# Routing the first half of the tokens first, and splitting the attention's weights inside the tile loop

## The reference

```python
x = x + 0.5 * ffn(layernorm(x), gate_w, expert_bias, w_up, w_down)
x = x + attention(layernorm(x), Wq, bq, Wk, bk, Wv, bv, Wo, bo)
x = x + 0.5 * ffn(layernorm(x), gate_w, expert_bias, w_up, w_down)
```

## Time and profile before

| what | value |
|---|---|
| three timed runs | 1325.23, 1333.52, 1334.07 us; median 1333.52 us |
| the profiled execution | 1327.57 us, its span 1325.8 us, granted clock 0.921 |
| TensorE busy | 926.0 us (70%) |
| VectorE busy | 1061.2 us (80%) |
| ScalarE busy | 677.8 us (51%) |
| GpSimd busy | 765.7 us (58%) |
| chain that ended last | VectorE 38%, TensorE 22%, GpSimd 15%, issue 15%, ScalarE 8% |

### The profile page before, as it was taken

One profiled execution on the slowest core, in us unless ns is written; L12 is line 12 of the kernel. 1 busy time (PEld: TensorE's weight loads), 2 busy tenths in 40 slices (PEclk: granted clock), 3 DMA queues, 4 the chain that ended last, 5 costly groups with the idle time before them and its releaser, 6 DMA issues.

```text
span 1325.8 us, 32789 instructions
## 1 busy us (share of the span) xinstructions
PE 926.0 (70%) x12808; PEld 753.3 (57%) x12808; DVE 1061.2 (80%) x2172; ACT 677.8 (51%) x950; POOL 765.7 (58%) x635
## 2 busy tenths in 40 slices
PE   4204978778876877877877887877978777767800
PEld 3203967666665655655655665655756567666700
DVE  7886766888899999899999998999998666447734
ACT  2113746556655655655655665645756464545500
POOL 2277627517767557557556564557978612766154
PEclk9999998999989999999999998988989888979865
DMA  9322424310000000000000000000000012233131
GB/s 331 128 92 88 126 68 106 84 45 6 10 6 7 8 6 8 7 6 7 8 6 2 2 2 2 2 2 17 14 13 14 29 53 69 85 113 100 54 87 52
DMA packets 69508, 61.77 MB, mean 47 GB/s; under 512 B 8304, under 2 KB 60016, under 8 KB 69104
## 3 DMA queue, kind: packets, MB, share of 16 engines
q1 hardware_dynamic: 60448, 42.64, 10.3%
q0 software_dynamic: 8192, 16.79, 4.1%
q10 hardware_dynamic: 720, 0.23, 0.1%
HBM read 30.80 MB, written 28.84 MB: 45 GB/s over the span
## 4 chain that ended last, share of the span: by engine, by line
DVE 38%; PE 22%; POOL 15%; issue 15%; ACT 8%; DMA 1%; DVEq 0%; POOLq 0%; ACTq 0%; SPq 0%
POOL xs L634 7%; DVE arena_a L1209 5%; DVE arena_c L1214 4%; PE bank L963 3%; DVE arena_b L1257 3%; ACT arena_b L1131 3%; DVE xn_new L424 2%; DVE arena_c L1273 2%; POOL arena_b L663 2%; PE bank L965 2%; PE bank L964 2%; PE bank L740 2%; DVE arena_c L1218 2%; PE bank L742 2%; PE bank L741 2%
## 5 line engine op out<-in xcount | busy, mean ns | idle before, releaser
L634 POOL DMA_INDIRECT xs<-xhl,slot_idx x128 | 154.5, 1207 | 102.7 <-issue 56.5
L800 ACT ACTIVATE arena_c<-bank,s_pre 128x1024 f32<-128x1024 f32 x92 | 102.6, 1115 | 204.0 <-PE bank L742 203.9
L1361 POOL TENSOR_TENSOR arena_a<-arena_a 128x1024 f16<-128x1024 f32 x64 | 139.0, 2171 | 55.5 <-ACT arena_a L1137 54.9
L1343 POOL TENSOR_TENSOR arena_a<-arena_b,trig_rows 128x512 f32<-128x512 f32 x128 | 160.1, 1271 | 6.8 <-issue 6.8
L825 DVE SCALAR_TENSOR_TENSOR arena_c<-arena_c,s_h 128x1024 f16<-128x1024 f32 x92 | 128.8, 1400 | 30.3 <-ACT arena_c L805 30.3
L1137 ACT ACTIVATE arena_c<-arena_a 128x1024 f16<-128x1024 f32 x64 | 67.6, 1057 | 164.3 <-DVE arena_a L1209 164.3
L663 POOL DMA_INDIRECT arena_b<-ys,slot_idx x96 | 106.9, 1113 | 75.5 <-DMA ys<-arena_b 47.9
L755 PE MATMUL bank<-wdn_hi,arena_c 128*128 x736 | 135.3, 226 | 20.1 <-DVE arena_c L825 20.1
L740 PE MATMUL bank<-arena_b,wup_hi 128*128 128x256 f16 x368 | 107.4, 292 | 59.2 <-DVE arena_b L821 59.2
L756 PE MATMUL bank<-wdn_hi,arena_c 128*128 x736 | 135.1, 226 | 0.0
L757 PE MATMUL bank<-wdn_lo,arena_c 128*128 x736 | 134.9, 225 | 0.0
(11 more groups left out here) (224 smaller groups left out, 3755.9 us busy)
## 6 DMA issues: line engine op xcount, KB each, us to landing
arena_b<-xs SPq DMA_DIRECT2D x92, 128.0 KB
ys<-arena_b SPq DMA_DIRECT2D x92, 128.0 KB
xs<-arena_c SPq DMA_DIRECT2D x2, 3072.0 KB, 18.4
arena_a<-in_w_up SPq DMA_DIRECT2D x1, 2048.0 KB, 13.0
arena_b<-in_w_down SPq DMA_DIRECT2D x1, 2048.0 KB, 13.5
xs<-xhl,slot_idx POOLq DMA_INDIRECT x128, 2.3
out_x<-x_tok SPq DMA_DIRECT2D x8, 256.0 KB, 2.6
arena_b<-ys,slot_idx POOLq DMA_INDIRECT x96
```

Source lines behind the costliest of these rows:

```text
L634: nc.gpsimd.indirect_dma_start(d["xs"][half], bass.IndirectOffsetOnAxis(slot_idx[:, half, choice, t:t + 1], axis=0), xhl[:, half, t, :], N ...
L1343: i = nc.gpsimd.tensor_tensor(q_trig[h], q_relu[h], trig_rows[:, bass.ds(u * BLK, BLK)], ALU.mult)
L1361: nc.gpsimd.tensor_tensor(q_lo, arena_a[:, 0:2 * BLK], q_hi, ALU.subtract).then_inc(a["q_lo_done"], 1)
```

## The change

1. In the prologue TensorE, ScalarE and VectorE take the first half's four blocks through transposes, gate products, split, gating and `route`, and then the second half's. `route_product(0)` writes to another PSUM bank, since the second half's logits lie in the old one.
2. The weights' largest values are taken on VectorE behind each half's route, no longer ahead of the gate; both low splits of the experts' weights follow the second half's route.
3. GpSimd reduces the up weights' largest values over the partitions behind 4 tiles of half 0's scatters (8 DMAs), those of the down weights behind 13 (26 DMAs), those of the attention behind all scatters of both halves.
4. The scale `s_y` is applied to the copied result of the down product, no longer to the gate's weights.
5. The attention's twelve pieces go into the tile loop of half 0, behind the low part of tiles 2, 4, 6, 8, 14, 15, 16, 17, 18, 19, 20 and 21. The rows of two biases are loaded into `arena_b` after the down weights are split, and TensorE waits for all logits ahead of `route_product(1)` only.

```diff
@@ buffers
-        bk_row, bv_row = take(HD), take(HD)
...
+        bk_row, bv_row = arena_b[:, 2 * HD:3 * HD], arena_b[:, 3 * HD:4 * HD]
@@ first_transpose
-            for n in range(NBLK):
-                pe.wait_ge(first_norm, n + 1)
...
-            for n in range(NBLK):
-                pe.wait_ge(first_hi, n + 1)
...
+            for half in range(2):
+                blocks = range(half * NBLK // 2, (half + 1) * NBLK // 2)
+                for n in blocks:
+                    pe.wait_ge(first_norm, n + 1)
...
+                for n in blocks:
+                    pe.wait_ge(first_hi, n + 1)
...
@@ first_copy, first_logits
-            for n in range(NBLK):
+            for n in range(half * NBLK // 2, (half + 1) * NBLK // 2):
@@ gating
-                then(nc.vector.scalar_tensor_tensor(w12[:, 0, tiles], col(2), s_y[:, 0:1], col(5), ALU.mult, ALU.mult))
-                then(nc.vector.scalar_tensor_tensor(w12[:, 1, tiles], col(4), s_y[:, 0:1], col(5), ALU.mult, ALU.mult))
+                then(nc.vector.tensor_tensor(w12[:, 0, tiles], col(2), col(5), ALU.mult))
+                then(nc.vector.tensor_tensor(w12[:, 1, tiles], col(4), col(5), ALU.mult))
@@ route_product, route
+        def ps_route(i):
+            return ps_tr if i else bank[0][:, 0, :]
@@ ffn_pe
                 route_product(pe, 0)
+                pe.wait_ge(gate_read, NBLK)
                 route_product(pe, 1)
@@ ffn_dve
-                nc.vector.tensor_copy(y_sb[G % 3].rearrange("p s f -> p (s f)"), ps_y[G % 2]).then_inc(f["y_used"], 1)
+                nc.vector.tensor_scalar(y_sb[G % 3].rearrange("p s f -> p (s f)"), ps_y[G % 2], s_y[:, 0:1], None, ALU.mult
+                                        ).then_inc(f["y_used"], 1)
...
                     if p < NPAIR:
                         low(G)
+                    if k == 0 and i == 0:
+                        if p in ATT_SETUP_TILES:
+                            attention_weights(v, ATT_SETUP_TILES.index(p))
@@ ffn_pool
-                scatter(g, 0, range(0, 10))
+                scatter(g, 0, range(0, 4))
+                reduce_largest(g, 0, 1, 0)
+                scatter(g, 0, range(4, 13))
+                reduce_largest(g, 1, 2, 1)
+                scatter(g, 0, range(13, HALF))
+                scatter(g, 1, range(0, HALF))
                 reduce_largest(g, 2, 9, 2)
-                scatter(g, 0, range(10, HALF))
-                scatter(g, 1, range(0, HALF))
                 add_input(g, 0)
                 add_input(g, 1)
@@ attention_weights
+        ATT_SETUP_TILES = (2, 4, 6, 8, 14, 15, 16, 17, 18, 19, 20, 21)
...
-                    v.wait_ge(in_att, 16 * 4)
+                    v.wait_ge(in_att, 16 * 6)
@@ sync
+            sp.wait_ge(w_dn_ready, 1)
+            for dst, name in ((bk_row, "bk"), (bv_row, "bv")):
+                sp.dma_start(dst, d[name].partition_broadcast(P)).then_inc(in_att, 16)
             ffn_sync(sp, 0)
@@ scalar
-            first_copy(act)
-            split_high(act, 0)
-            split_high(act, 1)
-            gating_exp(act, 0)
+            for half in range(2):
+                first_copy(act, half)
+                split_high(act, half)
+                gating_exp(act, half)
             expert_weights_high(act, W_UP)
-            gating_exp(act, 1)
             expert_weights_high(act, W_DOWN)
@@ gpsimd
-            reduce_largest(g, 0, 1, 0)
-            reduce_largest(g, 1, 2, 1)
             ffn_pool(g, 0)
@@ vector
-            v.wait_ge(in_up, 16)
-            largest_of(v, 0, arena_a[:], last=True)
-            scale_up(v)
-            v.wait_ge(in_dn, 16)
-            largest_of(v, 1, arena_b[:], last=True)
...
-            first_logits(v)
-            scale_down(v)
-            for i in range(2):
-                split_low(v, i)
+            for half in range(2):
+                first_logits(v, half)
+                split_low(v, half)
                 for j in range(GATE_PIECES):
-                    gating(v, i, j)
-                route(v, i)
-                expert_weights_low(v, (W_UP, W_DOWN)[i])
+                    gating(v, half, j)
+                route(v, half)
+                v.wait_ge((in_up, in_dn)[half], 16)
+                largest_of(v, half, (arena_a, arena_b)[half][:], last=True)
+                (scale_up, scale_down)[half](v)
+            expert_weights_low(v, W_UP)
+            expert_weights_low(v, W_DOWN)
-            for j in range(len(ATT_SETUP_SLOTS)):
-                attention_weights(v, j)
             ffn_dve(v, 0)
@@ tensor
             first_transpose(pe)
             pe.wait_ge(const_ready, 1)
-            pe.wait_ge(gate_read, NBLK)
             ffn_pe(pe, 0)
```

More of the change, by code:

```diff
@@ L214, in build @@
         route_raw = take(2 * NTABLE + E * NTILE // 2 + P)
-        bk_row, bv_row = take(HD), take(HD)
-        bias_part = take(HD, F16)
-        zeros = take(8 * P, F16)
+        bias_part = arena_c[:, 6144:6144 + HD // 2].bitcast(F16)
+        zeros = arena_c[:, 6144 + HD // 2:6144 + HD // 2 + 4 * P].bitcast(F16)
         take = carve(arena_b)
@@ L360, in first_transpose, with first_copy, first_logits @@
             pe.wait_ge(in_const, 16 * len(small))
-            for n in range(NBLK):
-                pe.wait_ge(first_norm, n + 1)
-                for t in range(TPB):
-                    i = nc.tensor.transpose(ps_first[n][:, t * P:(t + 1) * P], xnh[:, n * TPB + t, :], ident[:])
-                i.then_inc(first_tr, 1)
-            for n in range(NBLK):
-                pe.wait_ge(first_hi, n + 1)
[L368 to L373, removed]
-            for n in range(NBLK):
+            for half in range(2):
+                blocks = range(half * NBLK // 2, (half + 1) * NBLK // 2)
+                for n in blocks:
+                    pe.wait_ge(first_norm, n + 1)
+                    for t in range(TPB):
+                        i = nc.tensor.transpose(ps_first[n][:, t * P:(t + 1) * P], xnh[:, n * TPB + t, :], ident[:])
+                    i.then_inc(first_tr, 1)
+                for n in blocks:
+                    pe.wait_ge(first_hi, n + 1)
+                    for t in range(TPB):
+                        i = nc.tensor.matmul(ps_first[n][:, t * E:(t + 1) * E], first_xT32[n][:, t * P:(t + 1) * P],
+                                             gate_sb[:], start=True, stop=True)
+                    i.then_inc(gate_mm, 1)
+        def first_copy(act, half):
+            for n in range(half * NBLK // 2, (half + 1) * NBLK // 2):
                 act.wait_ge(first_tr, n + 1)
                 nc.scalar.activation(first_xT32[n], ps_first[n], ACT.Copy, scale=XSCALE).then_inc(first_hi, 1)
-        def first_logits(v):
-            for n in range(NBLK):
+        def first_logits(v, half):
+            for n in range(half * NBLK // 2, (half + 1) * NBLK // 2):
                 v.wait_ge(gate_mm, n + 1)
@@ L558, in route_product @@
             mask = rt_mask[:].rearrange("p e t -> p (e t)")
-            nc.tensor.matmul(ps_tr[:, 0:P], below_b[:], mask, start=True, stop=True)
-            nc.tensor.matmul(ps_tr[:, P:2 * P], ones_b[:], mask, start=True, stop=True).then_inc(route_mm, 1)
+            nc.tensor.matmul(ps_route(i)[:, 0:P], below_b[:], mask, start=True, stop=True)
+            nc.tensor.matmul(ps_route(i)[:, P:2 * P], ones_b[:], mask, start=True, stop=True).then_inc(route_mm, 1)
+        def ps_route(i):
+            return ps_tr if i else bank[0][:, 0, :]
         ROUTE_STEPS = 16
@@ L578, in route @@
             v.wait_ge(route_mm, i + 1)
-            then(nc.vector.tensor_copy(flat(rt_tot), ps_tr[:, P:2 * P]))
+            then(nc.vector.tensor_copy(flat(rt_tot), ps_route(i)[:, P:2 * P]))
             then(nc.vector.tensor_tensor_scan(flat(rt_incl), flat(keep), flat(rt_tot), 0.0, ALU.mult, ALU.add))
             nc.vector.tensor_scalar(rt_int[:], rt_incl[:, :, HALF - 1], float(2 * P - 1), None, ALU.add)
-            nc.vector.tensor_tensor(flat(rt_base), flat(rt_incl), ps_tr[:, 0:P], ALU.add).then_inc(route_read, 1)
+            nc.vector.tensor_tensor(flat(rt_base), flat(rt_incl), ps_route(i)[:, 0:P], ALU.add).then_inc(route_read, 1)
             v.wait_ge(route_read, i + 1)
@@ L1513, in build @@
                  (gbias[:], d["gbias"].partition_broadcast(P)))
-        tables = ((bk_row[:], d["bk"].partition_broadcast(P)), (bv_row[:], d["bv"].partition_broadcast(P)),
-                  (bo_row[:], d["bo"].partition_broadcast(P)), (bq_sb[:], d["bq2"]), (bkT_sb[:], d["bkT"]),
+        tables = ((bo_row[:], d["bo"].partition_broadcast(P)), (bq_sb[:], d["bq2"]), (bkT_sb[:], d["bkT"]),
                   (trig_rows[:], d["c_trig_rows"]), (trig_cols[:].rearrange("p g t -> p (g t)"), d["c_trig_cols"]),
```

2 lines of the change are left out of this document (removed).

## The result

The changed kernel takes **1346.35 us** (median, 1346.14 to 1350.56) against 1333.24 us for the kernel before on the same chip: ratio **1.0117, interval 1.0079 to 1.0154**. It is slower by 13.1 us; 14 were forecast. The profiled executions are 23 us apart (1350.56 and 1327.57), and the attention stage, which the change doesn't touch, differs by up to 10 us over the 14 traces of this case. So the stages are compared one by one.

What follows compares the result with a forecast made beforehand. Until 112.4 us GpSimd's scatters of half 0 set the end, then TensorE bounds the plain tile loop. Earlier start -6.5, loop +20.6 (6.2 + 13.4 + 1): +14 us; forecast 1343 us, range 1328 to 1358, 8 in 10.

Steps and rivals of the forecast that it cites:

- Start of the scatters: Prologue: routing begins earlier, so GpSimd's first scatter comes at 48.3 us, 11.0 us earlier than before.
- The configuration: GpSimd, before its first reduction, behind eight scatters: a change of configuration adds 7.2 us to the scatters' path.
- The rival in which it stays hidden: GpSimd's configuration is changed before the first scatter, in idle time: +7 us, 1336; chance 0.10.
- The rest up to the load: First scatter to first load of scattered rows: 53.05 us becomes 58.4; the load was taken at 106.
- SP's late loads: Two bias-row loads ahead of the tile loads on SP's queue, issued within 6 us before the load: cost nothing.
- VectorE's wait: Prologue: VectorE waits from 51.7 to 66.0 us for GpSimd's first reduction; all weights are ready at 99.9.
- the rival of a late wait: VectorE late at GpSimd's second reduction, so scatters stand behind it: costs its lateness, +18 us, 1348; chance 0.10.
- Sparse pieces and clock: Half 0's loop: four pieces at tiles 2, 4, 6, 8 cost 6.2 us; TensorE's halved clock adds 1 (0 to 3).
- Dense pieces: Half 0's loop, eight pieces at tiles 14 to 21: VectorE becomes the bound there, costing 13.4 us.
- The rival of half clock in the dense stretch: TensorE at clock 0.50 in tiles 14 to 21: up to 10 us more; +26 in all, 1355; chance 0.12.
- The additions: Additions of the input fall on tile 13 in place of 15: -1 to +4 us, if they reach the dense pieces.
- The rival that VectorE's idle time takes the pieces: Half 0's loop: 0.88 us idle a tile hides all but 8.1 of 28.3 us; +2, 1332; chance 0.18.

Runs made afterwards that it cites:

- the first experiment: The changed kernel plus an early, unused reduction over partitions on GpSimd at about 20 us; 1451.22 us (1.0101 of before) and 1446.32 us (1.0135).
- the pieces alone: The kernel before, own prologue order, with the attention's twelve pieces in half 0's loop, late bias loads and late third reduction; 1448.15 us, 1.0103 of before.
- the setup in gaps: The change with early reduction, attention setup in VectorE's waits and on ScalarE, five low parts in the loop; 0.999, 1.0006 and 0.9991 of before.

## Why the prediction was right, and where its terms were off

The forecast's mechanism held: an earlier start of 6.5 (measured 6.2), and more than that paid back in the loop, because TensorE was full and VectorE became the bound. (Its mean of 1330.1 and its sum of +14 make 1344, not 1343.) By steps:

**Start of the scatters.** Forecast 48.3, measured 46.31. Two terms make the 2 us. The 16 transposes took 3.65 us and not 4.5. And the second gate product took 3.96 us and not half of 13.47, since it met a spell of full clock. Half of 13.47 is the price at half the clock, and it held where the clock stayed there (7.00 us, first scatter at 47.31). The sum had no term for a clock that can be either; one of the two microseconds is luck of the execution.

**The configuration.** Forecast 7.2, measured 5.77; the first experiment shows that it stands where the first reduction stands. The back-change ahead of the additions took 6.98 (7.17 in the earlier trace rows); the two directions differ, and I had priced one by the other. The Trainium skill ("GPSIMD Engine Reference", 2.1 Instruction dispatch) says about 6 us, 5.95 measured, for the first call into freshly loaded code; the trace agrees. The rival in which it stays hidden is out.

**The rest up to the load.** From the first scatter to the load I took 57.7 (106 less 48.3) and it was 59.9, so that a start 2 us better and a way 2 us longer hid each other. Up to the issue of the last scatter the way is as reckoned, less what the configuration was dearer on paper: 50.7 us before, 5.4 more forecast, 54.9 measured. The excess lies behind it, and the term that was wrong is that of SP's late loads. I had them at nothing because SP's queue has time for them; what they take is time of the DMA engines. From the last scatter's issue to the first load it is 2.3 us in all six traces in which the attention's matrices and bias rows come early (both of before, the pieces alone with the bias rows at 81, the three of the setup in gaps). In the eight in which both come late it is 3.4 to 5.0: 5.0, 4.4 and 4.2 with the change, 3.5 with the early reduction. So late loads go with 1 to 2.7 us. Matrices and bias rows were never late one without the other, so which of them it is stays open.

**VectorE's wait** was 12.76 us to 62.5 (forecast: to 66). The down weights' largest values were ready at 83.7, GpSimd came to its second reduction at 87.28, 3.6 us later (forecast: 2), and VectorE waited 3.95 us for it. No scatter waited for VectorE: the rival of a late wait did not occur.

**The loop.** Forecast 20.6, measured 25.5:
- Sparse pieces and clock 10.5, forecast 7.2. Of them 3.1 are the first three tiles, 3.95 us each at a clock of 0.50 all the way to 122, where before has 1.00 from 119.8 on, 1 us into its first gelu. TensorE's half clock is the term that I had at 1 (0 to 3), and these tiles alone are over it. The remaining 7.4 I put down to the four largest-value pieces, forecast at 6.2 and at most 6.9; the clock was 0.50 from 129.2 to 132.7 too, so a part of it can be the clock's.
- Dense pieces 12.1 (35.27 less 8 x 2.9), forecast 13.4: they went as reckoned, VectorE back to back, and TensorE at a mean clock of 0.97. The rival of half clock in the dense stretch did not occur.
- The edge to the second half 1.8: 11.35 us from the 23rd to the 24th gelu in place of 9.59. Not foreseen.
- The additions fell on tiles 13 and 14 at 157.6, just as forecast, and cost 6.9 in place of 5.75: 1.1, in the range of -1 to +4.
- The result's copy, 0.48 us in place of 0.42 for each of 92 tiles, is in VectorE's idle time; the second half's loop (88.6 against 88.1) doesn't show it.

**The rival that VectorE's idle time takes the pieces** failed in the plainest way: 0.88 us a tile was idle, but ahead of the split and not behind it, where the pieces stood. The pieces cost 18.6 to 20.6 us of their 28.3.

**The sum** came out at +19.1 us at the 24th gelu against a forecast of +14, while the medians differ by 13.1. How much of the 6 us between them is the attention's own scatter can't be settled from two profiled executions: one of its lines (1257 before, 1270 after) takes 94.8 us in one and 107.7 in the other. On the other chips the medians differ by 17 to 18, as the 24th gelu does (17.0). So the loop's terms were 5 us low, and that the first chip's median falls within 1 us of the forecast difference is partly luck.

## What to carry to other kernels

Work that is hidden behind another engine's chain is not made cheaper by moving it into a loop, even one in which its engine shows idle time: ask which engine is full there, and whether the idle time lies behind the place where the work is put. Before moving, list the waits that the move itself opens; here a wait of 12.8 us (7.1 once the configuration was out of it), the time up to the load and an idle ScalarE took most of the setup, and the 19 to 21 us that the change had lost came back. A load that only has to wait its turn on a queue still takes the DMA engines from the transfer that everybody waits for. And a duration on TensorE is a price only together with its clock: the same product took 7.00 and 3.96 us in two executions of one kernel.

## What the runs showed that I had not expected

**Chips differ by 100 us in 1430** for one kernel, in places: only where GpSimd's indirect DMAs run beside the tile loop, with TensorE and VectorE standing 5 to 24 us at a time though nothing in the profile holds them. Four chips of five did this. That it is their instructions that come late behind the scatters is only a conjecture; no run separates it. It matters for reading a change: the lead at the load is not the lead at the 4th gelu. Same chip, 4.4 us became 2.7 (change and before), 5.7 became 3.4 (early reduction and change), and 12.8 became 15.6 (setup in gaps and before).

**The same 32 small f32 products took 6.83 us, and 3.96 directly afterwards**, at a granted clock of 0.50 and 1.00. In the 11 traces with the divided product the second part took 3.96 to 5.1 us in six, each with a record of 1.00 in that stretch, and 7.0 in five, which have no such record. So executions of one kernel differ in it, and the first scatter with them, by 1 us.

**A clock column of 1.00 can stand for no record.** In the first trace of the kernel before, the records of the granted clock begin at 119.8, and the profile's view gives 1.00 for any stretch ahead of that. Two stretches of it, each with 12 matmuls of 128x256 in f16:

```profile
116.20:118.50 2.30, 2.30 (x12) 1.67 (x11) 0.00 (x0) 0.00 (x0) 1.69 (x3) 1.00 0.35 114
120.00:121.30 1.30, 1.30 (x12) 1.14 (x13) 0.18 (x1) 1.09 (x1) 0.99 (x2) 1.00 0.48 151
```

The first tile's start 0.21 us apart, the second tile's 0.11: the kernel before too began its loop at half clock, and got the full one a tile later, at 119.8, where the changed kernel got it at 122.4, three tiles in. The pace of like matmuls tells what the column doesn't.
